# The relation edge stage of a graph kernel: the split of the scores woven between gathers and fade, four engines' orders changed

## The reference

```python
att = (q[edge_dst] * key_e).sum(-1) * rel_pri[edge_type] / sqrt(dk)
seg = edge_dst * r + edge_type            # a segment: one target node and one relation
amax = segment_max(att, seg)
ex = exp(att - amax[seg])
denom = segment_sum(ex, seg)
hsum = segment_sum((ex / denom[seg])[:, :, None] * val_e, seg)
```

## Time and profile before

| | |
|---|---|
| median of 3 runs | 4697.31 us (4695.75 to 4698.82) |
| profiled execution | 4715.45 us, its span 4713.6 us |
| busy over the span | PE 84%, DVE 83%, POOL 65%, ACT 58% |
| mean granted TensorE clock | 0.902 over the span, 0.82 in the relation stage |
| relation edge stage | 2224 to 4213 us of the span, 1989 us |

### The profile page before, as it was taken

The page is one execution under the profiler, slowest core; times in us unless marked ns, Lnnn a source line. Parts: engine busy times, 40 slices in busy tenths (PEclk is TensorE's granted clock), DMA queues, the critical chain, the costliest instruction groups (busy, mean ns, idle before and its releaser), DMA issues. The chain is left out here.

```text
span 4713.6 us, 110307 instructions
## 1 busy us (share of the span) xinstructions
PE 3947.5 (84%) x22800; PEld 3268.9 (69%) x22800; DVE 3890.3 (83%) x12033; ACT 2727.4 (58%) x8093; POOL 3043.5 (65%) x4136
## 2 busy tenths in 40 slices
PE   5888888888888879997888887887878888868877
PEld 2477777777777768996666666666666666648776
DVE  6799999999999965554778878788887887868887
ACT  5755555555555533332777777777777777752222
POOL 4588888888888811111667666666666767647776
PEclk9999999999999989998888888888888778879899
DMA  4687787787878856665777777777777777766564
GB/s 157 201 253 230 229 230 231 231 231 230 231 230 231 224 143 201 200 200 170 193 196 197 195 197 198 196 197 197 198 196 197 197 197 197 195 162 190 169 171 131
DMA packets 647403, 945.37 MB, mean 201 GB/s; under 512 B 215309, under 2 KB 490510, under 8 KB 647036
## 3 DMA queue, kind: packets, MB, share of 16 engines
q0 software_dynamic: 153792, 510.82, 38.1%
q1 hardware_dynamic: 493499, 433.36, 32.6%
HBM read 772.83 MB, written 171.02 MB: 200 GB/s over the span
## 5 line engine op out<-in xcount | busy, mean ns | idle before, releaser
L1431 POOL DMA_INDIRECT kv1c<-kv_table,rec x936 | 944.4, 1009 | 461.4 <-issue 394.5
L794 POOL DMA_INDIRECT kv<-kv_table,rec x864 | 843.9, 977 | 250.4 <-issue 234.4
L1494 ACT ACTIVATE wv<-kv1c,wv 128x64 f32<-128x64 f32 x3744 | 927.6, 334 | 16.4
L1558 DVE CUSTOM_DVE_ANT_0 masked_scores<-score_p,far 126x384 f32<-126x384 f32 x1248 | 621.0, 553 | 339.7 <-DMA kv<-kv_table,rec 266.7
L1651 PE MATMUL sum_p<-wv,hot 128*126 128x260 f32 x1872 | 679.6, 515 | 2.2 <-ACT wv L1494 0.9
L1615 PE MATMUL qe_p<-qrel,hotT 126*128 126x256 f32 x1872 | 578.4, 456 | 22.2 <-ACT hotT L1479 14.7
L961 PE MATMUL sum_p<-msg,hot 128*126 128x256 f32 x1728 | 434.2, 395 | 173.5 <-DVE msg L917 102.2
L1615 PEld LDWEIGHTS qe_p<-qrel,hotT 126*128 126x128 f32 x1872 | 459.0, 246 | 124.9 <-ACT hotT L1479 14.9
L895 DVE CUSTOM_DVE_ANT_0 qk<-qk,gates 128x256 f32<-128x256 f32 x864 | 526.8, 662 | 2.3 <-ACT gates L838 1.8
L1641 PE MATMUL peak_p<-peak,hotT 126*128 126x4 f32 x1872 | 285.1, 270 | 274.4 <-issue 195.6
L1651 PEld LDWEIGHTS sum_p<-wv,hot 128*126 128x126 f32 x1872 | 427.2, 244 | 101.3 <-issue 2.6
(11 more groups left out here) (247 smaller groups left out, 9165.1 us busy)
## 6 DMA issues: line engine op xcount, KB each, us to landing
key<-segment_keys SPq DMA_DIRECT2D x312, 189.0 KB
q_blk<-q_table SPq DMA_DIRECT2D x216, 192.5 KB
acc_table<-acc SPq DMA_DIRECT2D x312, 128.0 KB
qrel<-q_by_relation SPq DMA_DIRECT2D x312, 126.0 KB
acc_in<-acc_table SPq DMA_DIRECT2D x50, 767.8 KB
q_by_relation<-qrel SPq DMA_DIRECT2D x50, 756.0 KB
feat<-in_edge_feat_t SPq DMA_DIRECT2D x216, 128.0 KB
agg_table<-total SPq DMA_DIRECT2D x216, 126.0 KB
```

The source lines that it names most:

```text
L794: pool.indirect_dma_start(kv[k][:, t, :], None, c["kv0_d"], bass.IndirectOffsetOnAxis(ap=rec[k][:, t, 0:1].bitcast(I32), axis=0)).then_inc ...
L1431: pool.indirect_dma_start(kv[k][:, t, :], None, c["kv1_d"], bass.IndirectOffsetOnAxis(ap=rec[k][:, t, 0:1].bitcast(I32), axis=0)).then_inc ...
L1494: ins = act.activation(wv[k][:, t, h, 0:DK], kv[s][:, t, D + h * DK:D + (h + 1) * DK], ACT.Copy, scale=wv[k][:, t, h, DK:DK + 1])
L1558: dve.tensor_tensor_reduce(junk[k][:, h], score_p[:, :, h, :], far[it.slot(4)][:], 1.0, -BIG, ALU.subtract, ALU.max, top[s][:, h:h + 1]).t ...
```

## The change

The split is cut into four functions and the gathers into three, so that POOL's list can place them singly. In a step POOL now issues two gathers, the first cast of the split, the third gather, the first rest, the fade, the second cast and the last rest. DVE makes the scores before it takes the peak off, caps, and then does the maxima in three pieces (`maxima(0, 1)`, `maxima(2)`, `maxima(3)`) with `one_hot`, `old_peak` and `peak_drop` between them; `one_hot` runs one chunk later (lag 1 in place of 0). ACT makes the distances first and copies the turned parts last, behind the fade's exponential. PE turns the parts first and ends with the sum of the values (lag 4 in place of 5) and the queries (lag 0 in place of 1). Every instruction of before is still there, once per chunk, with the same operands.

```diff
--- before.py
+++ after.py
@@ -1421,17 +1421,19 @@
                 pool.wait_ge(filled, FILLS)
                 steps = chunk_steps(pool, c["steps1"])
 
-                def gather(it):
-                    k = it.slot(U)
-                    wait_slot(pool, loaded, it, LOADS)
-                    pool.sem_inc(held, 1)
-                    wait(pool, wv_ready, it, U)
-                    pool.sem_inc(held, 1)
-                    for t in range(T1):
+                def gather(t):
+                    def f(it):
+                        k = it.slot(U)
+                        if t == 0:
+                            wait_slot(pool, loaded, it, LOADS)
+                            pool.sem_inc(held, 1)
+                            wait(pool, wv_ready, it, U)
+                            pool.sem_inc(held, 1)
                         pool.indirect_dma_start(
                             kv[k][:, t, :], None, c["kv1_d"],
                             bass.IndirectOffsetOnAxis(ap=rec[k][:, t, 0:1].bitcast(I32), axis=0)
                         ).then_inc(gathered[k], 16)
+                    return f
 
                 def fade_acc(it):
                     s, last = it.slot(U), it.prev().slot(U)
@@ -1444,22 +1446,33 @@
                 def part(k, j):
                     return parts[k][:, :, j * HEADS:(j + 1) * HEADS]
 
-                def split_scores(it):
-                    k, n = it.slot(2), it.slot(4)
+                def first_part(it):
+                    k = it.slot(2)
                     hold(pool, held, score_ready, it.count())
                     wait(pool, partsT_turned, it, 2)
                     pool.sem_inc(held, 1)
-                    pool.tensor_copy(part(k, 0), score[n][:]).then_inc(split_ready, 1)
+                    pool.tensor_copy(part(k, 0), score[it.slot(4)][:]).then_inc(split_ready, 1)
+
+                def first_rest(it):
+                    k = it.slot(2)
                     pool.wait_ge(split_ready, it.count(1, 4, 1))
                     pool.sem_inc(held, 1)
-                    pool.tensor_tensor(rest[k][:], score[n][:], part(k, 0), ALU.subtract).then_inc(split_ready, 1)
+                    pool.tensor_tensor(rest[k][:], score[it.slot(4)][:], part(k, 0),
+                                       ALU.subtract).then_inc(split_ready, 1)
+
+                def second_part(it):
+                    k = it.slot(2)
                     hold(pool, held, split_ready, it.count(1, 4, 2))
                     pool.tensor_copy(part(k, 1), rest[k][:]).then_inc(split_ready, 1)
+
+                def third_part(it):
+                    k = it.slot(2)
                     pool.wait_ge(split_ready, it.count(1, 4, 3))
                     pool.sem_inc(held, 1)
                     pool.tensor_tensor(part(k, 2), rest[k][:], part(k, 1), ALU.subtract).then_inc(split_ready, 1)
 
-                run_chunks(pool, steps, ((5, fade_acc), (2, split_scores), (0, gather)))
+                run_chunks(pool, steps, ((0, gather(0)), (0, gather(1)), (2, first_part), (0, gather(2)),
+                                         (2, first_rest), (5, fade_acc), (2, second_part), (2, third_part)))
 
             @block.scalar
             def _(act):
@@ -1506,8 +1519,8 @@
                     wait(act, spread_ready, it, 2)
                     act.copy(partsT[it.slot(2)][:], partsT_p[:]).then_inc(partsT_ready, 1)
 
-                run_chunks(act, steps, ((4, weights), (4, weigh), (2, partsT_out), (0, distances), (0, transposed_hot),
-                                        (4, fades)))
+                run_chunks(act, steps, ((0, distances), (0, transposed_hot), (4, weights), (4, weigh), (4, fades),
+                                        (2, partsT_out)))
 
             @block.vector
             def _(dve):
@@ -1544,19 +1557,22 @@
                     dve.tensor_reduce(score[it.slot(4)][:], qk[it.slot(2)][:], AX, ALU.add).then_inc(score_ready, 1)
 
 
-                def maxima(it):
-                    k, s = it.slot(2), it.slot(U)
-                    wait(dve, spread_ready, it)
-                    dve.sem_inc(held, 1)
-                    wait(dve, far_ready, it)
-                    dve.sem_inc(held, 1)
-                    wait(dve, top_ready, it, 2, per=HEADS)
-                    dve.sem_inc(held, 1)
-                    wait(dve, peak_ready, it, U)
-                    dve.sem_inc(held, 1)
-                    for h in range(HEADS):
-                        dve.tensor_tensor_reduce(junk[k][:, h], score_p[:, :, h, :], far[it.slot(4)][:], 1.0, -BIG,
-                                                 ALU.subtract, ALU.max, top[s][:, h:h + 1]).then_inc(top_ready, 1)
+                def maxima(*heads):
+                    def f(it):
+                        k, s = it.slot(2), it.slot(U)
+                        if heads[0] == 0:
+                            wait(dve, spread_ready, it)
+                            dve.sem_inc(held, 1)
+                            wait(dve, far_ready, it)
+                            dve.sem_inc(held, 1)
+                            wait(dve, top_ready, it, 2, per=HEADS)
+                            dve.sem_inc(held, 1)
+                            wait(dve, peak_ready, it, U)
+                            dve.sem_inc(held, 1)
+                        for h in heads:
+                            dve.tensor_tensor_reduce(junk[k][:, h], score_p[:, :, h, :], far[it.slot(4)][:], 1.0, -BIG,
+                                                     ALU.subtract, ALU.max, top[s][:, h:h + 1]).then_inc(top_ready, 1)
+                    return f
 
                 def old_peak(it):
                     s = it.slot(U)
@@ -1598,8 +1614,9 @@
                     wait(dve, stored, it, U, per=16)
                     dve.tensor_tensor(acc[it.slot(U)][:], faded[it.slot(2)][:], sum_p[:], ALU.add).then_inc(acc_ready, 1)
 
-                run_chunks(dve, steps, ((2, q_times_k), (3, old_peak), (4, below_peak), (2, scores), (4, cap),
-                                        (3, maxima), (5, add_acc), (3, new_peak), (0, one_hot), (3, peak_drop)))
+                run_chunks(dve, steps, ((2, q_times_k), (2, scores), (4, below_peak), (4, cap), (3, maxima(0, 1)),
+                                        (1, one_hot), (3, old_peak), (3, maxima(2)), (4, peak_drop), (3, maxima(3)),
+                                        (5, add_acc), (3, new_peak)))
 
             @block.tensor
             def _(pe):
@@ -1652,8 +1669,8 @@
                                         start=t == 0, stop=t == T1 - 1)
                     ins.then_inc(summed, 1)
 
-                run_chunks(pe, steps, ((5, sum_values), (1, q_of_edges), (2, turn_parts), (3, peaks_of_edges),
-                                       (2, spread)))
+                run_chunks(pe, steps, ((2, turn_parts), (3, peaks_of_edges), (2, spread), (4, sum_values),
+                                       (0, q_of_edges)))
 
 
 def nodes_out(nc, c):
```

## The result

The change made the kernel slower: 4965.76 us against 4697.63 us, ratio 1.0565 (95% interval 1.0542 to 1.0587), 268 us more. The forecast was 4646 us in a range of 4585 to 4790; the time lies beyond the range on the slow side. The profiled execution of the changed kernel took 4956.61 us, its span is 4954.8 us.

The account below looks back on a forecast made before the run. POOL's own time was taken to set the 6.345 us step; afterwards the POOL-DVE loop through score would set 6.18, 0.165 less, times 312 steps 51 us: 4697 - 51 = 4646 us, range 4585 to 4790.

Parts of the forecast that it names:

- What bounds the kernel before: Relation stage: POOL runs without a stop and its own time sets the step of 6.37 us, though DVE is busier.
- the loop through the score: POOL and DVE form a two-step loop through score and cast: 12.36 us, 6.18 a step, binding by a little.
- The same eight instructions remain, so only gaps change: POOL's list by itself: changed gaps sum to 0.25 us a step less, 6.11, bounds 5.8 and 6.3.
- the gap before the first gather: POOL, between the split's last part and the first gather: taken as unchanged at 0.64 us.
- the sign: Whole kernel: faster, 4646 against 4697 us; chances 0.50 faster, 0.12 same, 0.38 slower.
- the blocking: Slower rival: DVE's hot and POOL's rest or fade hold each other, 0.8 us in two steps, 4770 us; chance 0.28.
- ACT's new order, hidden by 1.6 us of idle time: ACT: the drop's exponential ahead of the parts' copy costs nothing; without idle cover, 0.1 us a step and more.
- PE's list, at nothing: PE: the new list is a rotation with the same order in the steady loop, costed at nothing.
- The third gather's gap, 0.45 with bounds 0.15 and 0.64: POOL, between first cast and third gather: gap grows from 0.30 to 0.45 us, cost 0.15.
- The rival by which the maxima stay at 4.90: Slower rival: DVE's maxima still start 4.90 us after POOL's first gather; 6.83 a step, 4848 us; chance 0.06.

Follow-up runs that it names:

- e8: Kernel before, with POOL's fade moved between the first rest and the second cast, gathers still last: 4697.96 us, ratio 1.0000.
- e4: Kernel before with the whole new POOL list, the lists of DVE, ACT, PE and SP as before: 4939.65 us, ratio 1.0524.
- e1: Changed kernel with SP's store moved from lag 6 to lag 7: 4866.90 us, ratio 1.0360 to the kernel before.
- e9: Changed kernel, SP's store still at lag 6, with DVE's one_hot moved behind new_peak and old_peak behind q_times_k: 4955.13 us, ratio 1.0535.
- e7: e1 with DVE's one_hot moved behind new_peak and old_peak behind q_times_k: 4636.37 us, ratio 0.9873 to the kernel before.
- e2: Kernel before with SP's store moved from lag 6 to lag 7, nothing else: 4695.28 us, ratio 0.9999.
- e10: e1 with POOL's fade moved behind the last part of the split, DVE's order left alone: 4873.82 us, ratio 1.0356.
- e11: e7 with the two waits of POOL's first gather moved behind the fade: 4637.42 us, ratio 0.9859 to the kernel before.
- e12: e7 with DVE's four maxima in one piece and drop behind one_hot at lag 3: 4708.08 us, ratio 0.9997 to the kernel before.
- e6: Changed kernel with the gathers and ACT's distances and transposed one-hots at lag 1 in place of 0: 4991.70 us, ratio 1.0628.

## Why the prediction was wrong

- *What bounds the kernel before: right by the waits view, with less room than it seemed.* POOL waits for nobody there and DVE has slack. But e8 takes 0.2 us off POOL's list and gets it back as a wait for score: the loop through the score is nearly as long.
- *"The same eight instructions remain, so only gaps change", with the gap before the first gather kept at 0.64: this step failed, and with it the sign.* The wait of the gathers for SP's loads was put at nothing, without a reason; SP and its list don't occur in the prediction, and none of the rivals has them. The gathers' lag stayed 0 and their place went from last to first, which is one chunk further ahead. The loop acc, store, loads, gather, fade, acc went from three steps to two, and at 14.13 us it sets 7.07. The first gather waited 575 us for loads in 294 steps, 2.0 a step. e4 shows it without the blocking (7.05 a step, 4939.65 us), and e1 shows that a step more of lead for the loads over the store takes the wait away (-92 us).
- *ACT's new order, hidden by 1.6 us of idle time: incomplete.* Only the exponential of the drop was weighed. ACT's distances run one chunk ahead as well and waited 170 us for loads. PE's list, at nothing, is a rotation, and no run takes it apart.
- *The blocking of hot and fade: right in place, and given 0.28.* Its price was put at 0.8 us in two steps. Measured in e1, it is 0.67 of DVE's time in every step, because `old` behind `hot` is held too, by the fade that `hot` held. In the change itself, taking it away gives 4 us, inside the scatter (e9); in e1 the same edit gives 230. The page "SBUF — State Buffer" of the Trainium skill, section "Who interferes with whom", calls the pair of ports that DVE shares with GpSimd an exclusive lock, and says of DVE's two-port modes that who issues first has it for the whole instruction while the other blocks fully. e1's rows agree for the fade and for `old`, which ended 0.02 us after the fade. They don't for `hot`, which started before the rest and the fade and took 1.09 us all the same.
- *The third gather's gap, 0.45 with bounds 0.15 and 0.64: inside the bounds.* It is 0.16 in the change, at the lower one, 0.49 in most steps of e1 and 0.39 to 0.50 in most of e7.
- *The loop through score, 6.18 us a step: near, once the two other things are away.* e7 has 6.09 and takes 4636 us, where the forecast was 4646. That is partly luck: the maxima start 2.76 us after the first gather there (3006.12 against 3003.36) and not 3.6, and nine steps of about 8 us weigh against it. Nor is it shown that this loop sets e7's step: POOL waits for the score only 0.14 us a step there.
- *The rival by which the maxima stay at 4.90 fell.* In the turn shown they start at 3018.06, 0.89 us after the first gather, which itself was late. The 4.90 was no property of the lists either: e2 has the lists of DVE and POOL of before and its time, and no wait before the maxima at all; DVE waits before qk there.

## What to carry to other kernels

In a pipeline of in-order lists the lead of one function over another is its lag and its place together: moving a function from the end of a step to its front runs it a step ahead. So for each function that moves, write down which chunk it meets on every queue that feeds it, the loads' above all, and count over how many steps each loop closes. Two costs that don't lie in the same loop don't add: here one edit gave 4 us with the loads late and 230 us with the loads in time, and only both edits together made the new lists 1.3% faster than the old. And when a short two-input instruction of DVE is moved, look at what POOL runs at that moment, and at what stands behind each.

## What the runs showed of the hardware

- A held-up instruction passes it on: `hot` (0.61 us alone) holds the fade 0.30, the fade holds `old` 0.42 (means of e1). Which of two that meet is lengthened isn't settled by who started first alone: `hot` is, in e1, where it started before rest and fade; in e10 it isn't, and the rest is. Gathers are lengthened too: 0.95 to 1.23, up to 1.34 in e11, with `hot` running as they start. The section of the Trainium skill named above takes, as an inference, that a tensor-tensor instruction of DVE does not stall the making of descriptors; these rows don't agree, at least for this scalar-tensor-tensor form.
- Where DVE stands still differs between executions that take the same time. In the kernel before it waits in front of the maxima, which start 4.90 us after POOL's first gather and 2.4 us after the spread's end. In e2, with the same lists of both engines, nothing waits there, and DVE waits 204 us ("issue") and 70 us (the gathered rows) in front of qk. In e12 the wait before the maxima is back, at +3.41 in one turn (3006.03 against 3002.62), 2.4 us after a spread that ended at 3003.66. I have no mechanism for it and no run that isolates it.
- Once in 31 steps, nine times in the stage and some 190 us apart, the third gather of e7 comes 2.8 us late, as at 3014.62 ("issue"). The longest such wait is 2.8 in e1, e4, e6 and e9 to e12 too, and 1.0 before. An estimate of its cost in e7 is nine times 2.3 us (2.77 less the usual 0.49), some 20 us; its cause wasn't tried.
